# Attention and FFN layer on eight cores: the FFN weight's preparation moved into the loop over tiles, eight FFN tiles deferred

## The chip, the cores and the metric

The kernel runs on the eight cores of one Trainium2 chip. Each core does 4096 of the 32768 tokens and shares nothing with the others. The time is that of the device, in microseconds, of the slowest core.

## What is computed

A layer norm without weights, then attention over a window of seven neighbouring tokens with 16 heads of 64, and an FFN that is one product with a ternary weight; both are added to the input.

```python
def _layernorm(x, axis=-1, eps=1e-5): ...
def ste_quantize(w):
    scale = jnp.maximum(jnp.mean(jnp.abs(w)), EPS)
    return jnp.clip(jnp.round(w / scale), -1.0, 1.0)

xn = _layernorm(x, axis=-1)                       # x: (2, 16384, 1024) f32
# attention: q, k, v = xn @ w + b; 16 heads; each token sees offsets -3..3
scores = jnp.einsum('bhsd,bhskd->bhsk', q, k_win) * SCALE
attn = jax.nn.softmax(jnp.where(valid, scores, -jnp.inf), axis=-1)
out = jnp.einsum('bhsk,bhskd->bhsd', attn, v_win) @ w_o + b_o
# FFN: the scale is the mean of |weight|, a single number for the whole matrix
ffn = jnp.einsum('bsi,oi->bso', xn, w_ternary * scale)
x = x + out + ffn
```

## The kernel before

**Tiles and rings.** A core's 4102 rows (4096 and a margin of 3 on each side) are cut into 34 panels of 122 rows; a tile of 122 output rows needs a window of 128. Normalised, transposed activations `xnt`, keys `ktr` and queries `qme`, `qmo` (even and odd heads) are rings of four panels. `v_sb`, `ffn_sb`, `attok`, `atT`, `xr`, `osb` have two slots, `xl` (x for the layer norm) three. Five PSUM tensors: `p_tx` and `p_ta` for transposes, `p_qk` for all projections and for the FFN, `p_sc` for scores and attention output, `p_of` for the output projection. `p_qk` exists once, so each use waits for the evacuation of the last.

**Order.** The program is written out by hand: each `stage_` function appends instructions to five lists, one per engine, and each engine goes through its list in order. Waits are on counting semaphores; `evt` holds the count that an event reaches. The helper `dma(eng, chain, ...)` waits until the chain's earlier transfers have landed before it issues another, so one chain has one transfer in flight.

**Preamble.** SyncE loads three panels of x (122 rows of 4 KB each, 488 KB). Layer norm of panels 0 and 1 and the transposes of panel 0 follow. Then `emit_wcasts` loads wq, wk, wv, wo in 32 pieces of 512 KB over four slots of `wstage` and four chains, and ScalarE and VectorE cast them in turn. `emit_wf_prep` loads wf twice in four pieces of 1 MB: once for the sum of absolute values (L253), and, when the sum has gone over the partitions through two small matmuls (L266, L275), once for the ternary values, three VectorE instructions for each of eight blocks (L296, L300, L305), whose transposes (L313) and copies (L322) fill `wfT_b`. A row `brow` (bias of v through wo, plus bo) comes from 16 matmuls (L831). All this stands ahead of the loop in each engine's list.

**Loop.** Iteration s of 37 works on panel s and on tiles s-1, s-2 and s-3 in this order on TensorE: q and k projections of panel s (L475, bias L488), scores of tile s-1, heads 0 to 7 (L590), V projection of tile s-1 (L638), transposes of panel s+1 (L427) and of the attention output of tile s-2 (L666), scores, heads 8 to 15, FFN of tile s-1 (L692), output projection of tile s-2 (L721, L727), attention times V and row sums of tile s-1 (L748, L754). VectorE: reciprocals, `qmo` (L526), normalised attention (L779), residual addition `osb` of tile s-3 (L793), the mask multiplication `au_buf` (L614, one for each half of the heads), `xnt` (L441), part of the layer norm of panel s+2. ScalarE: `qme` (L522), `ktr` (L535), exponentials (L603), `v_sb` (L651), `atT` (L678), the rest of the layer norm, `ffn_sb` (L705). GpSimd adds `ffn_sb` to `osb` (L799) and stores it (L804). SyncE issues `xl` of panel s+3 (L336) and `xr`, the rows for the residual, of tile s-1 (L570); the latter waits for L793 of tile s-3.

## Time and profile before

| | us |
|---|---|
| median of 3 runs | 950.06 (949.19 to 950.79) |
| the profiled execution, its own time | 950.85 |
| its span, slowest core | 949.3 |
| spans of the eight cores | 941.7 to 949.3 |
| TensorE busy | 781.6 (82%) |
| VectorE, ScalarE, GpSimd busy | 324.7, 363.6, 98.9 |
| DMA, mean over the span | 77.07 MB, 81 GB/s |

The profile is of one execution on the slowest core. Its strip cuts the span into 40 slices of 23.7 us with the busy share of each in tenths. The chain of waits goes back from the last instruction to what released each step. The granted clock is given as a share of 2.4 GHz. A time in a row counts from the start of the span.

### The profile page before, as it was taken

To read this page: it belongs to the slowest core of one execution; us is meant where nothing else is said; L and a number is where in the kernel's file an instruction comes from. 1 tells how busy PE (TensorE), PEld (TensorE's weight loads), DVE (VectorE), ACT (ScalarE), POOL (GpSimd) and SP (SyncE) were. 2 spreads that over 40 slices of the span, in tenths; PEclk is the share of its full clock that TensorE was granted. 3 is DMA by queue.
4 is the path that set the end of the run, shared out by engine and by line. 5 is a ranking of instruction groups with operands and counts; after the bars stand their busy time and mean duration, and the time that the engine had idled before them with its cause. 6 is when DMAs were issued, how large, how long until landed. Compare 5 with 4: busy or idle time off the path is not lost.

```text
span 949.3 us, 21922 instructions; the slowest of 8 cores (941.7 to 949.3 us)
## 1 busy us (share of the span) xinstructions
PE 781.6 (82%) x8386; PEld 571.7 (60%) x8386; DVE 324.7 (34%) x566; ACT 363.6 (38%) x537; POOL 98.9 (10%) x72
## 2 busy tenths in 40 slices
PE   0000027899999999999999999999999999999984
PEld 0000014677777777777777777777777777777652
DVE  3112374223333333333333333333333333333221
ACT  0232113444444444444444444444444444444320
POOL 0000000001111111111111111111111111111112
PEclk9999999999999999999999999999999999999997
DMA  0479751101111111112211111111111111111211
GB/s 28 116 241 310 256 179 49 54 28 53 68 67 69 68 66 66 67 69 77 75 68 67 68 66 68 68 67 68 68 67 68 68 67 66 58 46 48 66 47 33
DMA packets 20531, 77.07 MB, mean 81 GB/s; under 512 B 1855, under 2 KB 1991, under 8 KB 20430
## 3 DMA queue, kind: packets, MB, share of 16 engines
q1 hardware_dynamic: 15582, 58.89, 17.4%
q0 software_dynamic: 4848, 16.78, 6.0%
q8 instruction: 70, 1.15, 0.5%
q14 instruction: 31, 0.25, 0.1%
HBM read 58.89 MB, written 16.78 MB: 80 GB/s over the span
## 4 chain that ended last, share of the span: by engine, by line
PE 80%; DMA 11%; DVE 4%; issue 2%; ACT 2%; DVEq 1%; POOL 0%; SPq 0%; ACTq 0%; POOLq 0%
PE p_qk L475 25%; PE p_of L727 13%; PE p_qk L692 13%; PE p_qk L638 13%; PE p_sc L748 5%; PE p_sc L590 3%; DMA xl<-x 3%; DMA wstage<-wq 2%; PE p_of L721 2%; PE p_qk L488 2%; DMA wstage<-wf 2%; PE p_qk L754 2%; PE p_tx L427 1%; DMA wstage<-wk 1%; DMA wstage<-wv 1%
## 5 line engine op out<-in xcount | busy, mean ns | idle before, releaser
L799 POOL TENSOR_TENSOR osb<-osb,ffn_sb 122x1024 f32<-122x1024 f32 (+1 forms) x34 | 80.1, 2355 | 822.8 <-DVE osb L793 803.5
L475 PE MATMUL p_qk<-xnt,wq_b 128*128 128x122 bf16 (+1 forms) x2176 | 128.2, 217 | 1.2 <-DVE xnt L441 1.2
L692 PE MATMUL p_qk<-wfT_b,xnt 128*122 128x512 bf16 (+1 forms) x544 | 123.6, 380 | 5.4 <-ACT v_sb L651 1.9
L727 PE MATMUL p_of<-wo_b,atT 128*122 128x512 bf16 (+1 forms) x544 | 126.7, 387 | 0.0
L638 PE MATMUL p_qk<-wv_b,xnt 128*128 128x512 bf16 (+1 forms) x544 | 124.6, 383 | 0.1
L475 PEld LDWEIGHTS p_qk<-xnt,wq_b 128*128 128x128 bf16 x2176 | 118.5, 98 | 9.0 <-issue 9.0
L475 PE MATMUL p_qk<-xnt,wk_b 128*128 128x122 bf16 (+1 forms) x2176 | 121.3, 215 | 0.4 <-ACT qme L522 0.4
L522 ACT CAST qme<-p_qk 64x488 bf16<-64x488 f32 (+1 forms) x86 | 39.2, 478 | 213.0 <-PE p_qk L488 205.8
L475 PEld LDWEIGHTS p_qk<-xnt,wk_b 128*128 128x128 bf16 x2176 | 115.7, 97 | 7.7 <-issue 7.6
L614 DVE TENSOR_TENSOR au_buf<-e_buf,mk_sb 128x976 bf16<-128x976 bf16 (+1 forms) x68 | 47.1, 693 | 207.4 <-ACT e_buf L603 207.4
L727 PEld LDWEIGHTS p_of<-wo_b,atT 128*122 128x122 bf16 (+1 forms) x544 | 70.5, 134 | 54.3 <-issue 16.0
L692 PEld LDWEIGHTS p_qk<-wfT_b,xnt 128*122 128x122 bf16 (+1 forms) x544 | 70.3, 134 | 48.9 <-issue 10.1
L638 PEld LDWEIGHTS p_qk<-wv_b,xnt 128*128 128x128 bf16 (+1 forms) x544 | 52.5, 99 | 57.3 <-issue 2.2
L266 PE MATMUL p_of<-stats,ones 128*1 128x1 f32 x2 | 0.2, 163 | 93.8 <-DVE stats L261 93.8
L603 ACT ACTIVATE e_buf<-p_sc,cst 128x976 bf16<-128x976 f32 (+1 forms) x68 | 71.8, 1056 | 7.5 <-PE p_sc L590 7.5
L535 ACT CAST ktr<-p_qk 128x488 bf16<-128x488 f32 (+1 forms) x86 | 39.7, 483 | 80.3 <-PE p_qk L475 80.3
L526 DVE CAST qmo<-p_qk 64x488 bf16<-64x488 f32 (+1 forms) x86 | 47.1, 565 | 64.8 <-PE p_qk L488 60.2
L748 PEld LDWEIGHTS p_sc<-v_sb,au_buf 128*122 128x122 bf16 (+1 forms) x544 | 63.1, 138 | 6.5 <-issue 3.9
L748 PE MATMUL p_sc<-v_sb,au_buf 128*122 128x64 bf16 (+1 forms) x544 | 64.4, 220 | 2.9 <-ACT ffn_sb L705 2.9
L651 ACT CAST v_sb<-p_qk 128x1024 bf16<-128x1024 f32 (+1 forms) x34 | 34.4, 1012 | 80.5 <-PE p_qk L638 80.5
L754 PE MATMUL p_qk<-ones128b,au_buf 128*122 128x1 bf16 (+1 forms) x544 | 64.3, 195 | 0.0
L754 PEld LDWEIGHTS p_qk<-ones128b,au_buf 128*122 128x122 bf16 (+1 forms) x544 | 62.4, 138 | 2.6
(77 smaller groups left out, 737.7 us busy)
## 6 DMA issues: line engine op xcount, KB each, us to landing
xl<-x SPq DMA_DIRECT2D x33, 488.0 KB
xr<-x SPq DMA_DIRECT2D x33, 488.0 KB
out<-osb POOLq DMA_DIRECT2D x33, 488.0 KB, 7.2
wstage<-wf SPq DMA_DIRECT2D x8, 1024.0 KB, 6.2
wstage<-wq SPq DMA_DIRECT2D x8, 512.0 KB, 11.6
wstage<-wk SPq DMA_DIRECT2D x8, 512.0 KB, 6.1
wstage<-wv SPq DMA_DIRECT2D x8, 512.0 KB, 5.6
wstage<-wo SPq DMA_DIRECT2D x8, 512.0 KB, 5.7
```

The source lines that it names most:

```text
L475: f = (lambda pp, m2, k2, c2, r2, wb2, st2, sp2: (lambda e: e.matmul(p_qk[0:128, c2:c2 + psz_of(pp)], wb2[0:128, k2 * H + 128 * m2: k2 * H ...
L522: f_e = (lambda pp, b2, qq, ww: (lambda e: e.copy(qap(qme)[0:64, 4 * b2:4 * b2 + 4, qq:qq + ww], p_qk[0:64, :].rearrange("p (b n) -> p b n ...
L526: f_o = (lambda pp, b2, qq, ww: (lambda e: e.tensor_copy(qap(qmo)[64:128, 4 * b2:4 * b2 + 4, qq:qq + ww], p_qk[64:128, :].rearrange("p (b ...
L535: f = (lambda pp, b2, rr, ww: (lambda e: e.copy(ktr_ap()[:, 4 * b2:4 * b2 + 4, rr:rr + ww], p_qk[:, :].rearrange("p (b n) -> p b n", b=2, ...
L603: inc("scalar", "s", (lambda ii, hf: (lambda e: e.activation(e_buf[0:wsz_of(ii), 8 * hf * TS:(8 * hf + 8) * TS] .rearrange("p (a b n) -> p ...
L614: inc("vector", "v", (lambda ii, hf, v2: (lambda e: e.tensor_tensor(au_buf[0:wsz_of(ii), :].rearrange("p (h n) -> p h n", h=NH, n=TS) [:, ...
L638: f = (lambda ii, k2, j2, r2: (lambda e: e.matmul(p_qk[0:wsz_of(ii), 512 * j2:512 * j2 + 512], xnt_ap()[:, k2, r2:r2 + wsz_of(ii)], wv_b[0 ...
L692: f = (lambda ii, k2, j2, q2: (lambda e: e.matmul(p_qk[0:tsz_of(ii), 512 * j2:512 * j2 + 512], xnt_ap()[:, k2, q2:q2 + tsz_of(ii)], wfT_b[ ...
L727: f = (lambda ii, k2, j2, a2: (lambda e: e.matmul(p_of[0:tsz_of(ii), 512 * j2:512 * j2 + 512], atT[:, :].rearrange("p (s c n) -> p s c n", ...
L748: f = (lambda ii, h2, v2: (lambda e: e.matmul(p_sc[0:tsz_of(ii), 64 * h2:64 * h2 + 64], au_buf[0:wsz_of(ii), TS * h2:TS * h2 + tsz_of(ii)] ...
L754: fd = (lambda ii, h2: (lambda e: e.matmul(p_qk[0:tsz_of(ii), 1008 + h2:1009 + h2], au_buf[0:wsz_of(ii), TS * h2:TS * h2 + tsz_of(ii)], on ...
L799: inc("gpsimd", "g", (lambda ii, s2, o2: (lambda e: e.tensor_add(osb[0:tsz_of(ii), o2 * H:(o2 + 1) * H], osb[0:tsz_of(ii), o2 * H:(o2 + 1) ...
```

## The change

Four things are changed together.

**Casts.** The 32 weight loads stay in one run on SyncE, with `xl` of panels 3 and 4 issued among them, after pieces 7 and 23. The casts go into the engines' lists at the start of iterations 0 (wq, wk), 1 (wv) and 2 (wo), on semaphores of their own (`cs`, `cv`). `brow` is made in iteration 2.

**wf.** Its preparation is cut into jobs, appended in iterations 3 to 7 behind the first half of the scores and the V projection: loads and absolute sums 0 and 1 in iteration 3, loads and sums 2 and 3 and the scale in iteration 4, blocks 0 and 1 in 5, blocks 2 to 4 in 6, blocks 5 to 7 in 7. The two small matmuls of the scale are replaced by four small transfers through a DRAM scratch tensor `scrv`, each in turn waited for.

**FFN of tiles 0 to 7.** It is taken out of iterations 1 to 8 and done in a run in iteration 8 (`flush_ffn_ladder`). `xnt` of tiles 0 to 4 is overwritten by then, so it is stored to DRAM (`scrx`, chain `x2`) in iterations 2 to 6 and loaded again into the space of `wtern`.

**Output of tiles 0 to 4.** Attention plus residual is stored to `out` in iterations 3 to 7 and in the run read back by GpSimd into `gsc` (under the name `pr_sb`), added to `ffn_sb` and stored again (`scr_pickup`).

```diff
+                jp = j - 4
+                wait("sync", "cs" if jp % 2 == 0 else "cv", jp // 2 + 1)
...
+                if j == 7 and NP > 3:
+                    stage_XLD(3)
+                    xld_done.add(3)
+                if j == 23 and NP > 4:
+                    stage_XLD(4)
+                    xld_done.add(4)
...
+            rng = {0: range(0, 16), 1: range(16, 24), 2: range(24, 32)}.get(s, range(0))
...
+        def _wf_scd1():
+            wait("sync", "v", evt[("wabs_c",)])
+            dma("sync", "sc", lambda e: e.dma_start(scrv_h[0, :], stats[:, 15:16]))
+            dma("sync", "sc", lambda e: e.dma_start(gsc[0:1, 0:128], scrv_h[0, :][None, :]),
+                key=("scd1",))
...
+        def _wf_scd2():
+            wait("sync", "v", evt[("srow",)])
+            dma("sync", "sc", lambda e: e.dma_start(scrv_h[1, :], gsc[0:1, 128:256]))
+            dma("sync", "sc", lambda e: e.dma_start(
+                sc_sc[:, 0:1], scrv_h[1, :].rearrange("(p n) -> p n", n=1)),
+                key=("scd2",))
...
+        S_F = min(8, NP + 2)
+        DEF = list(range(0, min(S_F, NT)))
+        SCR = list(range(0, max(0, S_F - 3)))
...
+        def emit_ffnev(j):
+            wait_ev("scalar", "t", ("ffn", j))
+            if j >= 2:
+                wait_ev("scalar", "s", ("ffnev", j - 2))
+                cons = ("ffnadd", j - 2) if (j - 2) in SCR else ("out2", j - 2)
+                wait_ev("scalar", "g", cons)
...
+        def x2_store(j):
...
+            dma("sync", "x2", (lambda jj, q2: (lambda e: e.dma_start(
+                scr_h[jj, :, :].rearrange("p (c n) -> p c n", c=8, n=TS),
+                xnt_ap()[:, :, q2:q2 + TS])))(j, qrc), key=("x2s", j))
...
+        def scr_pickup(jj):
+            wait_ev("gpsimd", "v", ("wtern", 7))
+            dma("gpsimd", "sp", (lambda j2: (lambda e: e.dma_start(
+                pr_sb[0:tsz_of(j2), :],
+                out_h[TS * j2:TS * j2 + tsz_of(j2), :])))(jj))
+            wait("gpsimd", "sp", 16 * (N_SCR + 2 * jj + 1))
+            wait_ev("gpsimd", "s", ("ffnev", jj))
+            inc("gpsimd", "g", (lambda j2: (lambda e: e.tensor_add(
+                pr_sb[0:tsz_of(j2), :],
+                pr_sb[0:tsz_of(j2), :],
+                ffn_sb[0:tsz_of(j2), (j2 % 2) * H:((j2 % 2) + 1) * H])))(jj),
+                key=("ffnadd", jj))
+            wait_ev("gpsimd", "g", ("ffnadd", jj))
+            dma("gpsimd", "sp", (lambda j2: (lambda e: e.dma_start(
+                out_h[TS * j2:TS * j2 + tsz_of(j2), :],
+                pr_sb[0:tsz_of(j2), :])))(jj))
...
+            for j in DEF:
+                if j - 2 in SCR:
+                    scr_pickup(j - 2)
...
+                if j >= 1:
+                    wait_ev("tensor", "s", ("ffnev", j - 1))
...
+            if s <= 2:
+                cast_flush(s)
...
+            flush_wf(s)
...
+            if s == S_F:
+                flush_ffn_ladder()
...
+            if 2 <= s <= S_F - 2 and (s - 2) in SCR:
+                x2_store(s - 2)
...
+                if ia >= S_F:
+                    stage_A_ffn(ia)
```

SyncE's list of before, from iteration 2 on, is a plain alternation; each xr waits for the VectorE addition two tiles back (`s_v`) and for its own predecessor (`s_lr`):

```order
50 L570 DMA xr<-x 122x1024 [waits s_lr]
51 L336 DMA xl<-x 122x1024 [waits s_s,s_v,s_lx]
52 L570 DMA xr<-x 122x1024 [waits s_v,s_lr]
53 L336 DMA xl<-x 122x1024 [waits s_s,s_v,s_lx]
54 L570 DMA xr<-x 122x1024 [waits s_v,s_lr]
```

Of the change, the same engine in iterations 3 and 4:

```order
46 L680 DMA xr<-x 122x1024 [waits s_v,s_lr]
47 L273 DMA wstage<-wf 128x2x1024 [waits s_cs,s_cv,s_w2]
48 L273 DMA wstage<-wf 128x2x1024 [waits s_cs,s_cv,s_w3]
49 L983 DMA scrx<-xnt 1024x1x122 [waits s_v,s_x2]
50 L442 DMA xl<-x 122x1024 [waits s_s,s_v,s_lx]
51 L680 DMA xr<-x 122x1024 [waits s_v,s_lr]
52 L273 DMA wstage<-wf 128x2x1024 [waits s_v,s_w2]
53 L273 DMA wstage<-wf 128x2x1024 [waits s_v,s_w3]
54 L297 DMA scrv<-stats 128x1 [waits s_v]
55 L298 DMA gsc<-scrv 1x128 [waits s_sc]
56 L315 DMA scrv<-gsc 1x128 [waits s_v,s_sc]
57 L316 DMA sc_sc<-scrv 128x1 [waits s_sc]
```

The loads of wf stand behind xr in the list, and the small transfers of the scale behind them.

VectorE before, one iteration from the residual addition to the layer norm:

```order
147 L793 TENSOR_TENSOR osb<-p_of,xr 122x1024 [waits s_t,s_lr,s_st,s_g]
148 L614 TENSOR_TENSOR au_buf<-e_buf,mk_sb 128x976 [waits s_s,s_t,s_v]
149 L441 COPY xnt<-p_tx 128x8x122 [waits s_t,s_v]
150 L367 TENSOR_REDUCE stats<-xl 122x1 [waits s_lx,s_v,s_s]
151 L372 TENSOR_SCALAR stats<-stats 122x1 [waits s_s]
```

The same place of the change, in iteration 5 (L920 is the residual addition, L724 the mask, L550 the xnt copy, L473 the sum of the layer norm):

```order
124 L920 TENSOR_TENSOR osb<-p_of,xr 122x1024 [waits s_t,s_lr,s_sp]
125 L724 TENSOR_TENSOR au_buf<-e_buf,mk_sb 128x976 [waits s_s,s_t,s_v]
126 L355 TENSOR_SCALAR gsc<-wstage,sc_sc 128x1024 [waits s_w2,s_v,s_sc]
127 L359 SCALAR_TENSOR_TENSOR gsc<-wstage,sc_sc,gsc 128x1024
128 L364 TENSOR_SCALAR wtern<-gsc,sc_sc 128x1024
129 L355 TENSOR_SCALAR gsc<-wstage,sc_sc 128x1024 [waits s_w2,s_v,s_sc]
130 L359 SCALAR_TENSOR_TENSOR gsc<-wstage,sc_sc,gsc 128x1024
131 L364 TENSOR_SCALAR wtern<-gsc,sc_sc 128x1024
132 L550 COPY xnt<-p_tx 128x8x122 [waits s_t,s_x2,s_v]
133 L473 TENSOR_REDUCE stats<-xl 122x1 [waits s_lx,s_v,s_s]
```

Between the mask and the xnt copy stand two ternary blocks, and ahead of them the wait for the load (`s_w2`).

GpSimd before did one addition and one store for each tile:

```order
7 L799 TENSOR_TENSOR osb<-osb,ffn_sb 122x1024 [waits s_v,s_s]
8 L804 DMA out<-osb 122x1024 [waits s_g,s_st]
```

In the run of iteration 8 it now has, after the reload of xnt, a read, an addition and a store for each of five tiles, all on the semaphore `s_sp`:

```order
13 L990 DMA wtern<-scrx 128x976 [waits s_t,s_x2,s_x3]
14 L1003 DMA gsc<-out 122x1024 [waits s_v,s_sp]
15 L1008 TENSOR_TENSOR gsc<-gsc,ffn_sb 122x1024 [waits s_sp,s_s]
16 L1014 DMA out<-gsc 122x1024 [waits s_g,s_sp]
17 L1003 DMA gsc<-out 122x1024 [waits s_v,s_sp]
18 L1008 TENSOR_TENSOR gsc<-gsc,ffn_sb 122x1024 [waits s_sp,s_s]
```

A read cannot be issued before the store ahead of it has landed.

## Rows read from the trace of the kernel before

**Rows 1.** The page's strip of 40 slices, TensorE matmuls, busy tenths.

```profile
PE   0000027899999999999999999999999999999984
```

**Rows 2.** Windows: length, busy of five engines, granted clock, DMA share, GB/s.

```profile
156.85:949.30 792.45, 766.36 (x8294) 562.45 (x8294) 269.59 (x490) 331.55 (x502) 98.73 (x68) 0.99 0.18 63
427.00:429.00 2.00, 2.00 (x26) 1.48 (x25) 0.00 (x0) 0.78 (x1) 0.00 (x0) 1.00 0.84 246
430.00:441.00 11.00, 11.00 (x99) 7.63 (x97) 2.49 (x8) 4.85 (x8) 0.00 (x0) 1.00 0.13 53
```

**Rows 3.** Chain of waits in order of time: start, duration, what.

```profile
1.06 1.95 DMA mk_sb<-mk
...
9.76 11.98 DMA xl<-x
...
35.31 17.74 DMA wstage<-wq
...
100.95 7.00 DMA wstage<-wf
...
156.85 1.82 PE p_qk L475 x32
...
213.70 1.74 PE p_qk L475 x32
...
236.24 1.74 PE p_qk L475 x32
```

**Rows 4.** Timeline up to 171 us: start, duration, instruction, idle before and its releaser.

```profile
75.47 0.69 DVE L227 CAST wk_b<-wstage 128x1024 bf16<-128x1024 f32 x1 [1.83 <-DMA wstage<-wk]
...
110.52 2.29 DVE L253 TENSOR_REDUCE absacc<-wstage 128x2 f32<-128x2048 f32 x1 [0.20 <-DMA wstage<-wf]
...
128.82 0.75 DVE L296 TENSOR_SCALAR gsc<-wstage,sc_sc 128x1024 f32<-128x1024 f32 x1
...
131.86 0.75 DVE L296 TENSOR_SCALAR gsc<-wstage,sc_sc 128x1024 f32<-128x1024 f32 x1
...
169.09 1.24 ACT L413 ACTIVATE xn_sb<-xl,stats 122x1024 bf16<-122x1024 f32 x1 [0.57 <-DVE stats L390]
```

**Rows 5.** Timeline and chain within one steady iteration, 416.5 to 439.

```profile
421.63 1.23 DVE L793 TENSOR_TENSOR osb<-p_of,xr 122x1024 f32<-122x1024 f32 x1
426.20 0.67 DVE L614 TENSOR_TENSOR au_buf<-e_buf,mk_sb 128x976 bf16<-128x976 bf16 x1 [3.34 <-ACT e_buf L603]
...
429.03 0.67 DVE L441 COPY xnt<-p_tx 128x976 bf16<-128x976 bf16 x1 [2.17 <-PE p_ta L666]
435.77 0.67 DVE L614 TENSOR_TENSOR au_buf<-e_buf,mk_sb 128x976 bf16<-128x976 bf16 x1 [2.64 <-ACT e_buf L603]
...
429.48 3.64 PE p_qk L692 x16
...
433.69 3.60 PE p_of L727 x16
```

**Rows 6.** Timeline of SyncE's own instructions, the DMA issues.

```profile
422.99 0.23 SPq L570 DMA_DIRECT2D xr<-x  x1
423.92 0.23 SPq L336 DMA_DIRECT2D xl<-x  x1
...
445.96 0.23 SPq L336 DMA_DIRECT2D xl<-x  x1
```

**Rows 7.** The page's GpSimd addition; DMA issues of 300 to 800, and 915 to 935.

```profile
L799 POOL TENSOR_TENSOR osb<-osb,ffn_sb 122x1024 f32<-122x1024 f32 (+1 forms) x34 | 80.1, 2355 | 822.8 <-DVE osb L793 803.5
...
out<-osb POOLq DMA_DIRECT2D x22, 488.0 KB, 7.2
...
out<-osb POOLq DMA_DIRECT2D x2, 488.0 KB, 3.9
```

**Rows 8.** The kernel's last tile: a window, columns as in rows 2, and the chain.

```profile
931.00:936.00 5.00, 4.34 (x10) 1.66 (x11) 0.00 (x0) 0.52 (x1) 2.88 (x2) 0.50 0.14 32
...
932.69 5.69 PE p_of L727 x16
```

More of the change, by code:

```diff
@@ L233, in emit_wf_prep @@
[L233 to L246 removed]
+        wf_state = {"wfT": -1, "ffnev": -1, "tat": -1}
@@ new lines, in _mk_p1ld, with _mk_wabs, f @@
+            return f
+        def _mk_wabs(j):
+            def f():
+                slot = j % 2
+                wait("vector", _wf_chain(j), evt[("wld", j)])
+                inc("vector", "v", (lambda sl, kk: (lambda e: e.tensor_reduce(
+                    absacc[:, 2 * kk:2 * kk + 2],
+                    wstage[:, 2 * sl * H:(2 * sl + 2) * H].rearrange("p (c n) -> p c n", c=2, n=H),
+                    AX.X, ALU.add,
+                    apply_absolute_value=True)))(slot, j), key=("wabs", j))
+            return f
@@ L328, in build_program, with flush_wf @@
+        for _c in range(2, 4):
+            _wfj(6, _mk_tern(_c))
+            _wfj(6, _mk_wtr(_c))
+        _wfj(6, _mk_p2ld(3))
+        _wfj(6, _mk_tern(4))
+        _wfj(6, _mk_wtr(4))
+        for _c in range(5, 8):
+            _wfj(7, _mk_tern(_c))
+            _wfj(7, _mk_wtr(_c))
+        wf_ptr = [0]
+        def flush_wf(s):
+            while wf_ptr[0] < len(wf_jobs) and wf_jobs[wf_ptr[0]][0] <= s:
+                wf_jobs[wf_ptr[0]][1]()
+                wf_ptr[0] += 1
         stash_P = {}
@@ L849, in build_program @@
             ir = s - 3
-            if s + 3 < NP:
+            if s + 3 < NP and s + 3 not in xld_done:
                 stage_XLD(s + 3)
+            if s <= 2:
+                cast_flush(s)
             if 0 <= io < NT:
```

449 lines of the change are left out of this document (281 added, 168 removed).

## The prediction, on record before the changed kernel ran

> **What bounds the kernel now.** I read the page's strip of slices first [rows 1]: TensorE is nearly idle in the first six of forty slices and full from the eighth on. The windows [rows 2] put the border at 156.85 us; from there TensorE is busy 766 of 792 us, so the loop is bound by its matmuls. The chain of waits [rows 3] then gives the calendar. Call the start of the projections of iteration s P(s). P(0) is at 156.85, P(3) at 213.70, P(4) at 236.24: the period is 22.54 us, so P(9) is at 213.70 + 6 x 22.54 = 348.9, and 600.4 us follow it. The hole before P(0) is what the change attacks. Its reason is in the timeline [rows 4]: the casts of wq and wk end at 76.2 us, yet P(0) stands behind wv, wo, two passes over wf and eight ternary blocks.
>
> Next I look at what is not on the path today but becomes so, the DMA queue of SyncE. The first xl load of 122 rows, alone, takes 11.98 us [rows 3]; 12.1 with the wake of the engine behind it is what I use. The windows [rows 2] say why: in 430 to 441 us the DMA share is 0.13, two of 16 engines, at 53 GB/s. A 488 KB load occupies these two for 10.4 to 11 us. xl and xr go out together once per period and follow one another on the same two engines: the issues of xl at 423.92 and 445.96 are 22 us apart [rows 6], and an issue waits for its predecessor to land. That pair of engines is busy 21 of 22.5 us, and whatever SyncE issues over all 16 engines finishes only after its two shares have passed the same line. The wq load behind the third xl shows it: 17.74 us for 512 KB [rows 3].
>
> **The change, part by part.** I work out the new P(s), on the profiled execution (950.85 us, span 949.3).
>
> (a) P(0). It now waits for wq and wk only, 76.2 us. But xl 3 is put between their loads, and costs its two engines 10.4 us in a stream that keeps all 16 busy. P(0) = 86.6: **-70.3 us**. The bounds are 76.2 and 88.3 (the 12.1 us).
>
> (b) Iterations 0 to 2. The casts of wv stand on ScalarE and VectorE ahead of the evacuations of P(1), and need loads that wait for casts that now stand behind LN of panel 2. Before, LN 2 ended at 170.33, 13.5 us after P(0) [rows 4]; 15.5 where P(0) begins at half clock. Four casts, four loads of about 1.7 us after a 5 us latency: the last cast is at +26, and the k projection, which needs the evacuated q bank, starts only then. P(2) comes at about +47. Loads of wo go behind xl 4 (10.4 us on the two engines), land at +36 to +41, and the last four are asked for at +46: cast at +56. The bias row (16 matmuls, an addition on VectorE) stands ahead of the output projection: P(3) at +80. Before it was 56.9: **+23.1**. Bounds: 0 if the casts' loads are always there in time, 30 if the restarts cost more.
>
> (c) Iterations 3 to 7. These have no FFN matmuls (3.64 us each) [rows 5], but that is worth little. Behind the V projection a chain runs through other engines: xnt at 429.03, LN, the second exp, au done at 436.44 [rows 5]. TensorE's own work, with the FFN, ends at 437.29. Without it the chain is what is late, and an iteration is 21.7, not 18.9. Times with a plus count from P(s); in [rows 5] P(s) is 236.24 + 8 x 22.54 = 416.5. Behind an obstacle on VectorE that ends at D, the chain is xnt to au, 7.4, and attnV, 1.8 (437.29 to the next P at 439.0): 9.3. Where transposes, a copy of wfT and the copy of atT behind it come between, I estimate 12.4. After a stall of over 2 us TensorE restarts at half clock: the granted clock is 0.50 (1.2 GHz) from 931 on, after a wait of 2 us, and 16 matmuls take 5.69 [rows 8] where the same 16 take 3.60 [rows 5]. With the few around them I take 2.7 us per restart. In each of these iterations SyncE issues xr after the residual addition (done at +6.4 [rows 5]), then 1 or 2 MB of wf at +6.9, behind xr on the two engines. So the first megabyte lands at 6.9 + 12.1 + 2.5 = +21.5, the second at +24.0 (2.5 apart, as the wf pair of before that landed at 107.95 [rows 3] and by 110.52 [rows 4]).
> - Iteration 3: xr 0, xl 5, xr 1, xl 6 and xr 2 all queue from +54 after P(0), 5 x 10.4 and the first x2 store of 2: the wf pair lands 113 and 115 after P(0), the second abs sum ends at 117, P(3) + 37. With 9.3 and 2.7: 49.0.
> - Iteration 4: abs sum done at 24.0 + 2.3 + 0.2; then two round trips through DRAM, four small transfers at 1.95 each [rows 3] and 1.2 of VectorE, all waited for on VectorE: 35.5. Iteration 47.5.
> - Iteration 5: 21.5 and two ternary blocks of 3.04 [rows 4], for which TensorE waits too, since the transposes stand in its order: 27.6 + 12.4 + 2.7 = 42.7.
> - Iteration 6: the third block needs a load issued in it, 24.6: 39.7. Iteration 7: three blocks from +10.5: 34.8.
>
> Sum 213.7 against 5 x 22.54: **+101.0**.
>
> (d) Iteration 8, the ladder. Eight FFN tiles stand in a row, from +12.9 on (V projection and v_sb). Each needs p_qk free, so each evacuation waits for its predecessor; and from the third on the evacuation waits for a slot of ffn_sb, so for GpSimd to have read the tile two before back from DRAM, added and begun the store. One buffer, one semaphore: read, add, store, in series. The add is 2.36 us [rows 7]; for the handovers I estimate 0.8. The store is 7.2 us with xl and xr about, 3.9 at the end of the kernel with that queue empty [rows 7]. After some 18 us of ladder the queue is empty, so I take 3.9, for the read too: a period of 11.0. The first pickup is issued at about +10 (after two small reloads), its addition ends at +19.6, the fifth at +63.8. Then evacuation 6, tile 7 at half clock (6.8 us): the ladder leaves TensorE at +72. Txn, LN, exp, au and attnV at the cold clock again: +84. P(9) = P(8) + 96.9 against 22.5: **+74.4**; 29 us of it is matmul work that left the eight earlier iterations, where it was mostly cover.
>
> The x2 stores (250 KB in short runs), the stores of tiles 0 to 4 and the reloads have slack of an iteration; I cost them at 2 us on the two engines in (c), and elsewhere at nothing. If a store took 10 us, the xnt copy behind it would wait: up to 5 x 8 us more. For (c) and (d) the bounds are the rivals 1 to 3 below.
>
> Sum: -70.3 + 23.1 + 101.0 + 74.4 = +128.2. P(9) at 477, and from there all is as before. 950.85 + 128 = 1079, and 0.8 less for the median of before: **1078 us**.
>
> **A rule beside it.** The trace shows 122-row loads on two engines. The Trainium skill, DMA: Bandwidth & Descriptors, section on why a DMA increments its semaphore by 16, says that a DMA uses the largest count up to 16 that divides its slowest dimension; for 122 that is 2, and the trace agrees. It also says that on GpSimd's path some direct copies use all 16 all the same: the out stores do (246 GB/s and a share of 0.84 while one moves, in 427 to 429 us [rows 2]). Which of the two the new read of out follows, no row shows.
>
> **The rivals.**
> 1. The wf loads do not stand behind xr. For it: the first wf load of before lands 7.00 us after its issue at 100.95 [rows 3]; nothing in the loop of before shows a 16-engine load behind an xr. Against: the wq load of 17.74 us. Then iterations 3 to 7 take 31, 40, 35, 35 and 35 us, 38 less, and (a) loses its 10.4: 1030.
> 2. The pickup read runs on two engines like xl: 12.1 instead of 3.9. Four periods of 8.2 more and 5 on the first: 38 more, 1116. The skill's page named above leaves room for it.
> 3. The pickups stay at 7.2 each way: 4 x 6.6 = 26 more, 1104.
> 4. Faster than before: TensorE is never held by the moved work, because VectorE (idle two thirds of the loop) does it in gaps. Then only (a) and (b) count, -47: 904. It decides where the extra of iterations 3 to 8 falls below 47 us. I find 175. VectorE alone needs 34 us for sums and blocks, TensorE waits for each block in order, and four pickup periods are 44 with only 24 of matmuls beside them. The whole mechanism would have to be a different one.
>
> **How the numbers follow.** Forecast, 1053 to 1103: 0.56. Rival 1: 0.17. Rival 2: 0.12. Rival 3: 0.08. Something between 953 and 1020, still slower: 0.04. Rival 4: 0.03. The range 1028 to 1110 leaves out rival 2, the unnamed rest and rival 4, 0.19. About 0.2% is what a measurement of this kernel can tell: faster 0.03, same 0.01, slower 0.96.
>
> **What would show it.** P(0) (first q projection after the wk casts) near 87 us, with an xl load among the weight loads. VectorE idle for 10 us or more ahead of each absacc reduction and of the first gsc of iterations 5 and 6, released by the wf DMA; a landing of wf near 15 to 17 us after issue, not 7. Two waits of 4 us for scrv. In the ladder TensorE at 0.50, ScalarE's ffn_sb copies released by GpSimd, 11 us apart. P(9) near 477 and then a period of 22.5. Wrong would be: wf landing in 7 us (rival 1), pickups 19 us apart (rival 2), or a loop after P(9) with another period, which no part of this allows for.

## The result and the profile after

The changed kernel takes **1106.7 us** (median of 10 runs, 1101.8 to 1113.0); the kernel before took 949.6 beside it (10 runs, 948.5 to 951.1). The ratio is **1.1655, interval 1.1631 to 1.1679**: slower by 157 us. Forecast was 1078 with 1028 to 1110 around it. The direction is right, the size is 29 us short, and the time lies in the upper end of the range. The times here and below leave out executions in which the cores of one die ran at a lower clock than the others. The profiled execution took 1103.6 us; its slowest core has a span of 1102.1, the others 1087.3 to 1101.0.

The page's strip, TensorE busy and granted clock in 40 slices of 27.6 us, and the page's line on the wf loads:

```profile
PE   0005586432384783569999999999999999999984
...
PEclk9999688675785897679999999999999999999987
...
wstage<-wf SPq DMA_DIRECT2D x8, 1024.0 KB, 18.7
```

TensorE works from slice 4 on, where before it began in slice 6 [rows 1], but it is about half idle until slice 19, and its mean clock is lower in most of these slices. From slice 19 on the strip is that of before. A megabyte of wf lands 18.7 us after its issue (median), where 7.00 stood in the chain before [rows 3].

The calendar comes from VectorE's timeline. The reciprocal of tile s-2 starts within 0.4 us of P(s), so I take its starts as the starts of iterations 2 to 10:

```profile
142.18 0.25 DVE L893 RECIPROCAL recip<-p_qk 122x16 f32<-122x16 f32 x1
166.55 0.26 DVE L893 RECIPROCAL recip<-p_qk 122x16 f32<-122x16 f32 x1 [4.32 <-PE p_qk L878]
212.20 0.26 DVE L893 RECIPROCAL recip<-p_qk 122x16 f32<-122x16 f32 x1 [3.86 <-PE p_qk L878]
271.68 0.26 DVE L893 RECIPROCAL recip<-p_qk 122x16 f32<-122x16 f32 x1 [3.86 <-PE p_qk L878]
317.64 0.26 DVE L893 RECIPROCAL recip<-p_qk 122x16 f32<-122x16 f32 x1 [2.34 <-PE p_qk L878]
360.50 0.26 DVE L893 RECIPROCAL recip<-p_qk 122x16 f32<-122x16 f32 x1 [3.57 <-PE p_qk L878]
393.20 0.26 DVE L893 RECIPROCAL recip<-p_qk 122x16 f32<-122x16 f32 x1 [2.34 <-PE p_qk L878]
496.84 0.26 DVE L893 RECIPROCAL recip<-p_qk 122x16 f32<-122x16 f32 x1 [3.26 <-PE p_qk L878]
521.57 0.26 DVE L893 RECIPROCAL recip<-p_qk 122x16 f32<-122x16 f32 x1 [2.75 <-PE p_qk L878]
```

Set against the forecast, step by step:

| | forecast | measured |
|---|---|---|
| P(0) | 86.6 | 85.9 |
| P(3) after P(0) | 80 | 80.7 |
| iterations 3, 4, 5, 6, 7 | 49.0, 47.5, 42.7, 39.7, 34.8 | 45.7, 59.5, 46.0, 42.9, 32.7 |
| iteration 8 | 96.9 | 103.6 |
| P(9) | 477 | 496.8 |
| from P(9) to the end of the span | 600.4 | 605.3 |

The chain of waits (start, duration, what) shows what the long iterations are made of:

```profile
62.24 14.92 DMA wstage<-wk
...
85.89 3.41 PE p_qk L585 x32
...
177.66 20.99 DMA wstage<-wf
...
220.76 19.12 DMA wstage<-wf
...
242.60 9.91 DMA scrv<-stats
...
252.58 3.60 DMA gsc<-scrv
...
257.26 1.12 DMA scrv<-gsc
...
258.44 1.95 DMA sc_sc<-scrv
...
280.45 17.18 DMA wstage<-wf
...
324.30 18.22 DMA wstage<-wf
...
417.39 8.02 DMA gsc<-out
...
433.03 4.58 DMA gsc<-out
...
478.48 6.51 PE p_qk L805 x16
```

Each of iterations 3 to 6 has one wf load of 17 to 21 us in the chain. In iteration 4 the four small transfers of the scale follow it. From 417 on it is the pickups: read, addition, store, read. The view of waits for 200 to 500 us (total, times, longest) names the same three obstacles from the side of the engines that wait:

```profile
PE p_sc L872 <- DVE au_buf L724: 62.6, 3, 36.6
...
ACT ffn_sb L821 <- POOL gsc L1008: 57.4, 5, 12.2
...
PE p_ta L379 <- DVE wtern L364: 40.6, 8, 16.1
...
DVE gsc L355 <- DMA wstage<-wf: 23.0, 2, 13.9
```

Its first line holds TensorE's longest waits, for the mask `au_buf`: 36.6 us in iteration 4 and 24.0 in iteration 3, because the second mask of an iteration stands in VectorE's list behind the xnt copy, and that one behind the absolute sums and the scale. TensorE also waits 41 us for ternary blocks, and VectorE, ahead of those blocks, for wf. ScalarE waits 57 us for GpSimd before it may copy the next FFN tile out of `p_qk`, five times. In iterations 3 to 7 together TensorE is busy 120 of 227 us, at a mean clock of 0.71 (columns as in [rows 2]):

```profile
166.55:393.20 226.65, 119.82 (x1209) 89.72 (x1207) 72.49 (x109) 53.66 (x77) 3.89 (x7) 0.71 0.27 80
```

### The profile page after: what moved, and what is told of

Its sections match the earlier page's. It is cut to its first block, busy times and chain, and to the rows that moved or that the text cites. A ratio compares the mean times of both kernels' runs of the same rounds, so it can differ in the third digit from the quotient of the medians.

```text
span 1102.1 us, 22136 instructions; the slowest of 8 cores (1087.3 to 1102.1 us)
## 1 busy us (share of the span) xinstructions
PE 819.4 (74%) x8382; PEld 595.7 (54%) x8382; DVE 323.9 (29%) x567; ACT 364.8 (33%) x537; POOL 106.8 (10%) x87
## 4 chain that ended last, share of the span: by engine, by line
PE 64%; DMA 21%; DVE 4%; issue 4%; ACT 3%; POOL 2%; DVEq 1%; SPq 1%; ACTq 0%; POOLq 0%
PE p_qk L585 21%; PE p_of L850 11%; PE p_qk L748 9%; PE p_qk L805 9%; DMA wstage<-wf 7%; PE p_sc L872 4%; DMA gsc<-out 2%; DMA wstage<-wq 2%; DMA xl<-x 2%; DMA wstage<-wk 2%; PE p_sc L700 2%; PE p_of L844 2%; PE p_qk L598 2%; PE p_qk L878 2%; POOL gsc L1008 1%
## 5 line engine op out<-in xcount | busy, mean ns | idle before, releaser
L585 PE MATMUL p_qk<-xnt,wq_b 128*128 128x122 bf16 (+1 forms) x2176 | 137.4, 225 | 62.1 <-DVE wk_b L251 57.3
L585 PEld LDWEIGHTS p_qk<-xnt,wq_b 128*128 128x128 bf16 x2176 | 127.5, 102 | 70.5 <-issue 70.4
L850 PE MATMUL p_of<-wo_b,atT 128*122 128x512 bf16 (+1 forms) x544 | 132.6, 400 | 0.0
L805 PE MATMUL p_qk<-wfT_b,xnt 128*122 128x512 bf16 (+1 forms) x464 | 112.5, 398 | 23.8 <-ACT ffn_sb L821 19.3
L872 PE MATMUL p_sc<-v_sb,au_buf 128*122 128x64 bf16 (+1 forms) x544 | 68.4, 225 | 69.6 <-DVE au_buf L724 69.4
L934 POOL TENSOR_TENSOR osb<-osb,ffn_sb 122x1024 f32<-122x1024 f32 (+1 forms) x28 | 65.9, 2354 | 518.2 <-DVE osb L920 499.0
L724 DVE TENSOR_TENSOR au_buf<-e_buf,mk_sb 128x976 bf16<-128x976 bf16 (+1 forms) x68 | 46.5, 684 | 210.1 <-ACT e_buf L713 210.1
L805 PEld LDWEIGHTS p_qk<-wfT_b,xnt 128*122 128x122 bf16 (+1 forms) x464 | 62.9, 141 | 65.9 <-issue 35.4
L878 PE MATMUL p_qk<-ones128b,au_buf 128*122 128x1 bf16 (+1 forms) x544 | 68.2, 198 | 0.0
L645 ACT CAST ktr<-p_qk 128x488 bf16<-128x488 f32 (+1 forms) x86 | 39.7, 483 | 84.5 <-PE p_qk L585 84.5
L878 PEld LDWEIGHTS p_qk<-ones128b,au_buf 128*122 128x122 bf16 (+1 forms) x544 | 66.3, 145 | 2.2
L550 DVE COPY xnt<-p_tx 128x976 bf16<-128x976 bf16 (+1 forms) x34 | 22.5, 661 | 141.3 <-PE p_tx L533 139.1
## 6 DMA issues: line engine op xcount, KB each, us to landing
wstage<-wf SPq DMA_DIRECT2D x8, 1024.0 KB, 18.7
```

Source lines behind the costliest of these rows:

```text
L585: f = (lambda pp, m2, k2, c2, r2, wb2, st2, sp2: (lambda e: e.matmul(p_qk[0:128, c2:c2 + psz_of(pp)], wb2[0:128, k2 * H + 128 * m2: k2 * H ...
L645: f = (lambda pp, b2, rr, ww: (lambda e: e.copy(ktr_ap()[:, 4 * b2:4 * b2 + 4, rr:rr + ww], p_qk[:, :].rearrange("p (b n) -> p b n", b=2, ...
L724: inc("vector", "v", (lambda ii, hf, v2: (lambda e: e.tensor_tensor(au_buf[0:wsz_of(ii), :].rearrange("p (h n) -> p h n", h=NH, n=TS) [:, ...
L805: f = (lambda ii, k2, j2, q2: (lambda e: e.matmul(p_qk[0:tsz_of(ii), 512 * j2:512 * j2 + 512], xnt_ap()[:, k2, q2:q2 + tsz_of(ii)], wfT_b[ ...
L850: f = (lambda ii, k2, j2, a2: (lambda e: e.matmul(p_of[0:tsz_of(ii), 512 * j2:512 * j2 + 512], atT[:, :].rearrange("p (s c n) -> p s c n", ...
L872: f = (lambda ii, h2, v2: (lambda e: e.matmul(p_sc[0:tsz_of(ii), 64 * h2:64 * h2 + 64], au_buf[0:wsz_of(ii), TS * h2:TS * h2 + tsz_of(ii)] ...
```

## The experiments

Two theories go in. The first is the prediction's: the x loads of 122 rows occupy two DMA engines, and wf, which uses all sixteen, finishes behind them; without FFN matmuls the chain through LN and the second exponential is late; the pickups go in series. The second stands for its rivals: that wf is slow for another reason, that the FFN matmuls left a real gain in iterations 3 to 7, and that the pickups are held by two slow engines. Differences below are differences of the ratios to the runs of before beside them, times 950 us.

**Experiment 1.** In the changed kernel every x load, `xl` and `xr`, is issued as 112 and 10 rows.

```diff
-            dma("sync", "lx", (lambda pp, s2: (lambda e: e.dma_start(
-                xl[0:psz_of(pp), s2 * H:(s2 + 1) * H],
-                x_h[TS * pp:TS * pp + psz_of(pp), :])))(p, p % 3),
+            for rn in (16 * (psz_of(p) // 16), psz_of(p) % 16):
+                if rn:
+                    inc("sync", "lx", (lambda pp, s2, a, n: (lambda e: e.dma_start(
+                        xl[a:a + n, s2 * H:(s2 + 1) * H],
+                        x_h[TS * pp + a:TS * pp + a + n, :])))(p, p % 3, r0, rn),
```

> The change, with each 122-row load of x (xl and xr) issued as two, 112 rows and 10 rows, and nothing else altered. Queue theory (122 rows run on two engines, and wf waits behind them): a load of x lands in about 4 us, the three first ones no longer hold the weights, P(0) moves from 86 to about 53, wf lands 7 to 8 us after its issue instead of 19, iterations 3 to 6 lose some 12 us each, and the time falls by about 90, to near 1017. Rival (the wf loads were slow for another cause, such as traffic of the other cores or the scattered stores of xnt): x loads may land sooner, but wf stays near 15 to 19 us and the time falls by less than 40.

Measured: ratio 1.0969 (1.0919 to 1.1020), 1043 us, 65 less. P(0) came at 58.4 instead of 85.9, and iterations 3 to 7 took 198 us instead of 227. Of the page, the wf loads:

```profile
wstage<-wf SPq DMA_DIRECT2D x8, 1024.0 KB, 10.3
```

So the two-engine loads are the cause of most of what the 18.7 us had above 7, and of 27 us ahead of P(0). They are not all of it: 90 us less and a landing of 7 to 8 were expected, and the landing went to 10.3. Two loads of 1 MB are still issued behind an `xr`, and their volume has to pass.

**Experiment 2.** The change with the wf loads issued at the top of each iteration, ahead of `xl` and `xr`.

```diff
+        top_jobs = {3: [_mk_p1ld(0), _mk_p1ld(1)], 4: [_mk_p1ld(2), _mk_p1ld(3)],
+                    5: [_mk_p2ld(0), _mk_p2ld(1)], 6: [_mk_p2ld(2)]}
...
-            _wfj(3, _mk_p1ld(_j))
...
+            for _f in top_jobs.get(s, []):
+                _f()
             if s + 3 < NP and s + 3 not in xld_done:
```

> The change, with the wf loads of iterations 3 to 6 (all but the last) issued by SyncE at the top of the iteration, ahead of xl and xr instead of behind xr. Queue theory: they are issued about 7 us sooner and no xr of the same iteration stands ahead of them, so in iterations 4 to 6 wf is in when VectorE comes to it at +10.5 and these give back 10 to 14 us each; iteration 3 gives back less, since older xl and xr are still queued: 30 to 50 us less in all, near 1065. Rival (wf is slow for a cause of its own): 7 us less at most in each of four iterations, under 28 in all.

Measured: 1.1203 (1.1170 to 1.1237), 1064 us, 43 less. Iterations 3, 5 and 6 fell to 25.8, 32.8 and 33.5; iteration 3, expected to give back least, gave back most. The landing of wf fell from 18.7 to 12.2 us (the page's median). But the edit did more than change the order in the queue. In the changed kernel SyncE comes to wf only when `xr` ahead of it may be issued, which waits for the residual addition; at the top of the iteration it is held by nothing of that iteration. The first pairs went out at 157.24 and 183.59, which is 10 us before P(3) and P(4), instead of 7 to 8 us after them. That is 17 to 18 us earlier and not the 7 of the expectation, so the bound of 28 us for the rival doesn't hold, and this run can't tell the place in the queue from the earlier issue. Experiment 1, which leaves the order alone, can. Iteration 4 rose to 65.2; its chain says why:

```profile
209.57 24.86 DMA scrv<-stats
...
234.50 1.51 DMA gsc<-scrv
...
238.19 9.16 DMA sc_sc<-scrv
```

What now stands behind `xl` (issued at 195.1) and `xr` (201.0) on the two engines is the first small transfer of the scale, half a kilobyte. Part of the 24.86 us is its own: in the changed kernel the same transfer took 9.91, with a DMA share of 0.01 beside it. The 9.16 us of the last transfer stand on this core only; on the other seven it took 1.9 to 2.0.

**Experiments 3, 9 and 12** ask what the absent FFN matmuls are worth in the loop, in the kernel before. All three leave out 14 of the 16 FFN matmuls of every tile. Experiment 3 does nothing else:

```diff
-            for kc in range(8):
+            for kc in (0,):
```

> The kernel before, with 2 of the 16 FFN matmuls of each tile left (the other 14 are left out, so the FFN output is not computed in full). My reading of iterations without FFN (the chain V projection, LN, exp, au is what is late): taking 14 x 0.227 = 3.2 us of matmul out of each iteration shortens the period from 22.54 to 21.7 only, and a wait of TensorE for au_buf of over 2 us appears ahead of the attention products. Rival (TensorE's own work is what counts): the period falls to about 19.4, and the time by 34 x 3.2 = 108 us.

Measured: 980.7 us in one run, against 950.9 for the kernel before (median of six runs). Some 108 us of TensorE's work are gone (14 of 16 matmuls of 3.64 us [rows 5], 34 times), and the kernel is **slower by 30 us**. Neither theory had that. One iteration, chain of waits:

```profile
427.35 3.02 PE p_qk L475 x32
...
446.89 1.06 ACT e_buf L603
...
448.18 0.68 DVE au_buf L614
...
449.20 0.21 PE p_sc L748
```

VectorE's copy of xnt in the same iteration, from its timeline, and TensorE's wait for the mask in the whole run:

```profile
441.43 0.67 DVE L441 COPY xnt<-p_tx 128x976 bf16<-128x976 bf16 x1 [2.16 <-PE p_ta L666]
```

```profile
PE p_sc L748 <- DVE au_buf L614: 71.4, 30, 2.8
```

TensorE now waits some 2.4 us in each iteration for the second exponential and the mask. The next 32 matmuls take 3.02 us where they took 1.74 before [rows 3], at a granted clock of 0.53, nearly all at 1.2 GHz (window of 427.35 to 430.40). The period is 23.8 us, 2.1 above the prediction's 21.7: xnt starts 14.1 us after the iteration and not 12.5 (1.3 of the 1.6 is the restart), and attention times V takes 2.3 after the mask and not 1.8. The chain between the two is 7.4 as forecast. In the kernel before, the FFN matmuls fill this gap.

Experiment 9 puts the second exponential ahead of the layer norm in the lists:

```diff
                 stage_O_tat(io)
+            if 0 <= ia < NT:
+                stash_sc2.pop(ia)(1)
             if s + 2 < NP:
...
-                stash_sc2.pop(ia)(1)
                 stage_A_ffn(ia)
```

> The kernel before with 2 of 16 FFN matmuls (as e3; the other 14 are left out) and the second exponential and its mask multiplication ahead of the layer norm of panel s+2 in the lists of ScalarE and VectorE, in every iteration. In e3 the period was 23.8 us, above the 22.54 with all matmuls: TensorE waited 2 us for au_buf ahead of attnV in each iteration and did the next 32 matmuls at half clock (3.0 instead of 1.8 us). Chain theory: with the exponential first, au_buf is ready some 5 us sooner, the wait and the half clock go, and the period falls to what the matmuls take, about 19.3: a time near 950 - 34 x 3.2 = 842. Rival (the clock falls for another cause, such as less work per iteration): the period stays above 22.

Measured: 1023 us in the profiled execution, a miss by 180. TensorE waited 100 us in 31 waits for the copy to `ffn_sb`. The chain of an iteration:

```profile
482.23 1.10 ACT e_buf L603
...
488.90 1.00 ACT ffn_sb L705
...
490.04 0.21 PE p_sc L748
```

The exponential is early as meant, but the copy to `ffn_sb` was left behind the layer norm, and the row sums of the attention (L754) write to `p_qk`, which this copy frees. I had looked at one tenant of the buffer only. Experiment 12 moves both:

```diff
+            if 0 <= ia < NT:
+                stash_sc2.pop(ia)(1)
+                stage_A_ffn(ia)
             if s + 2 < NP:
...
-            if 0 <= ia < NT:
-                stash_sc2.pop(ia)(1)
-                stage_A_ffn(ia)
```

> As e9 (2 of 16 FFN matmuls; the other 14 are left out), with the two matmuls and the copy to ffn_sb ahead of LN as well. In e9 the exponential was no longer late, but the copy to ffn_sb was behind LN on ScalarE, and attnV waits for it because both use p_qk: the wait grew from 2 to 5 us and the period to 25. Chain theory: with nothing that attnV needs behind LN, the wait before it goes, TensorE stays at full clock and the period is what the matmuls take, 19.3 to 19.8: a time of 840 to 860. Rival (fewer matmuls per iteration lower the clock or expose another chain): the period stays above 21.

Measured: 853.4 us in one run, against 951.8 beside it. Two reciprocals of its loop:

```profile
442.56 0.26 DVE L769 RECIPROCAL recip<-p_qk 122x16 f32<-122x16 f32 x1 [1.32 <-PE p_qk L754]
462.27 0.26 DVE L769 RECIPROCAL recip<-p_qk 122x16 f32<-122x16 f32 x1 [1.33 <-PE p_qk L754]
```

The period is 19.71 us, near TensorE's own 22.54 - 3.64 = 18.9 and two matmuls; the mean clock of the slowest core is 0.987 instead of 0.933. Same arithmetic, 127 us apart from experiment 3: with the lists as they were, the chain and the clock behind it, not the matmuls, set an iteration without FFN.

**Experiment 4.** The edit of experiment 1 alone in the kernel before.

> The kernel before, with the same two-part loads of x and nothing else altered. Queue theory: the three x loads at the start take about 4 us each instead of 12, the third no longer stands ahead of the weights, and the weights come about 24 us sooner; all behind them in the preamble is a chain, so P(0) moves from 157 to about 132 and the time falls by about 24, to near 926. The loop does not change, since its x loads have slack. Rival (the first 34 us are a start-up cost of the memory, not of the two engines): less than 5 us.

Measured: 0.9799 (0.9773 to 0.9824), 931 us. The start of the first projections moved from 156.85 to 137.85 us, 19 where 24 were expected; the period stayed at 22.5. The windows (columns as in [rows 2]) of before:

```profile
14.00:20.00 6.00, 0.00 (x0) 0.00 (x0) 5.14 (x9) 0.00 (x0) 0.00 (x0) 1.00 0.13 53
20.00:26.00 6.00, 0.00 (x0) 0.00 (x0) 1.82 (x6) 3.02 (x5) 0.00 (x0) 1.00 0.09 29
```

and of this run:

```profile
14.00:20.00 6.00, 0.00 (x0) 0.00 (x0) 5.15 (x2) 0.00 (x0) 0.00 (x0) 1.00 0.35 90
20.00:26.00 6.00, 0.00 (x0) 0.00 (x0) 3.45 (x15) 4.24 (x7) 0.00 (x0) 1.00 0.95 258
```

In 14 to 20 us x is being loaded in both; the DMA share goes from 0.13 (two of sixteen) to 0.35, and from 20 us on the weights already have nearly all sixteen. The rule that the prediction quoted (the Trainium skill, DMA: Bandwidth & Descriptors, section Why a DMA increments its semaphore by 16 and not by 1) would give 112 rows sixteen engines; the trace agrees that they are more than two, and in a window of large and small loads doesn't show their number. The 19 us lie in the preamble alone, since in the loop of before nobody waits for x.

**Experiment 5.** The change with the five reads of `out` issued ahead of the run of FFN tiles, each into its own buffer and on its own semaphore; GpSimd then only adds and stores.

```diff
+        def scr_read(jj):
...
+            dma("gpsimd", pk_ch[jj], (lambda j2: (lambda e: e.dma_start(
+                pk_buf(j2),
+                out_h[TS * j2:TS * j2 + TS, :])))(jj), key=("pkr", jj))
...
+                for jj in SCR:
+                    scr_read(jj)
```

> The change, with the five reads of out issued by GpSimd right after the two x2 reloads of iteration 7, each into a buffer of its own (four slots of wstage, free by then, and gsc) with a semaphore of its own; additions and stores as before, no store waited for. Serial-pickup theory: the 12.2 us period of the run of FFN tiles goes; each tile takes its 3.64 of matmul and 1.1 of evacuation, and iteration 8 falls from 103.6 to about 65 to 70: 34 to 38 us less in all. Rival (the run is held by the reloads of xnt, 5.8 us each, and by half clock): 15 us less or fewer.

Measured: 1.1304 (1.1281 to 1.1328), 1074 us, 33 less. Iteration 8 took 69.1 us instead of 103.6. ScalarE's copies out of `p_qk`, in its timeline:

```profile
434.20 1.01 ACT L822 COPY ffn_sb<-p_qk 122x1024 f32<-122x1024 f32 x1 [5.13 <-POOL wstage L1019]
439.30 1.01 ACT L822 COPY ffn_sb<-p_qk 122x1024 f32<-122x1024 f32 x1 [4.09 <-PE p_qk L800]
```

These two are 5.1 us apart, 16 matmuls and a copy, and all eight 5.0 to 7.1, where the changed kernel has 12.0 to 13.2 from the second to the seventh. The serial pickup is confirmed as the price of iteration 8. What is left, 69 us against 22.5, is the run of eight tiles over one `p_qk` and the chain behind it.

**Experiment 6.** The scale by two matmuls as before, instead of through DRAM.

```diff
-            dma("sync", "sc", lambda e: e.dma_start(scrv_h[0, :], stats[:, 15:16]))
...
+            inc("tensor", "t", lambda e: e.matmul(
+                p_of[0:1, 8:9], ones128[:, 0:1], stats[:, 15:16], start=True, stop=True),
+                key=("abs_mm",))
```

> The change, with the scale made by the two small matmuls of the kernel before (in iteration 4, into p_of) instead of the four transfers through DRAM. Iteration 4 took 59.5 us; from the last absolute sum (242.3) to the scale on all partitions (260.8) it spent 18.5, where the kernel before spent 1.9 (122.3 to 124.2). Theory: 16 to 17 us less in all. Rival (the wait only uncovers another): less than 8.

Measured: 1.1509 (1.1461 to 1.1556), 1092 us, 14 less. Iteration 4 fell from 59.5 to 47.0, 12.5 where 16 to 17 were expected. The same step in its chain, two matmuls instead of four transfers:

```profile
247.39 0.20 PE p_of L299 x2
...
247.98 0.55 PE p_of L308 x2
```

**Experiment 7.** The four transfers kept, but the first vector of 128 floats is written with 512 bytes from one to the next.

```diff
+    scrp_h = nc.dram_tensor("scrp", [128, 128], F32, kind="Internal").ap()
...
-            dma("sync", "sc", lambda e: e.dma_start(scrv_h[0, :], stats[:, 15:16]))
+            dma("sync", "sc", lambda e: e.dma_start(scrp_h[:, 0:1], stats[:, 15:16], allow_slow_non_contiguous=True))
```

> The change, with the 128 numbers of the first scale transfer written 512 bytes apart in DRAM (and read back from there as 128 single numbers) instead of next to each other. In the change that write of 512 bytes took 9.91 us and the read of it 3.60. If the write is slow because 128 writes of 4 bytes fall into one short stretch of DRAM, it falls to 3 us or less here; if it is slow for being 128 writes of 4 bytes wherever they go, it stays near 10. The read will be 3 to 5.

Measured: 1098.9 us in one run. The write's place in the chain:

```profile
243.78 1.44 DMA scrp<-stats
```

1.44 us instead of 9.91, with the same number of 4-byte pieces and the same place in the list. The other cores repeat it: 1.4 to 2.5 us on the eight cores of this run, 6.2 to 9.9 on those of the changed kernel. Iteration 4 took 52.3 instead of 59.5. The write is slow when the 128 pieces fall into one stretch of 512 bytes. What in the memory does that, the run doesn't tell. The Trainium skill, DMA: Bandwidth & Descriptors, section Specifications, says that a transfer below 512 bytes is a read-modify-write; that would hold for both layouts, so it can't be the difference by itself.

**Experiment 10.** The repairs of experiments 1, 5 and 6 together.

> The change with the repairs of e1 (x loads in two parts), e5 (reads of out ahead) and e6 (scale by matmuls) together. If the three costs are separate they add: 1107 - 62 - 33 - 15 = 997, still slower than before, since the DVE work inside iterations 3 to 7, the missing cover of the FFN and half clock remain. If they overlap (each repair was worth more because another wait was there) the sum is smaller: above 1010.

Measured: 1.0521 (1.0486 to 1.0556), 1000 us. The three single gains are 65 + 33 + 14 = 112, together they give 108: they are nearly independent. By its calendar (P(3) 136.9, P(8) 322.1, P(9) 395.8 against 213.8, 326.5, 349.1 of before) the early start is 77 us ahead at P(3), iterations 3 to 7 give back 73 and iteration 8 another 51. With each of the three found costs repaired, the plan still loses 50 us: from P(3) to P(8) TensorE is busy 121 of 185 us at a mean clock of 0.75, and its longest waits there are still for ternary blocks (29 us) and for the mask (17).

**Experiments 8 and 11** ask rival 4: is moving the preamble into the loop wrong, or this way of doing it? Both defer the FFN of three tiles only, so that no tile goes through DRAM, put all casts into iteration 0 and wf into iterations 0 to 3, and take the repairs of experiments 1 and 6. The second exponential stands ahead of the layer norm while the FFN is deferred.

```diff
-        S_F = min(8, NP + 2)
+        S_F = 3
...
-            rng = {0: range(0, 16), 1: range(16, 24), 2: range(24, 32)}.get(s, range(0))
+            rng = {0: range(0, 32)}.get(s, range(0))
...
+            (0, "E"): [_mk_wabs(0), _mk_p1ld(2), _mk_wabs(1), _mk_p1ld(3)],
+            (1, "A"): [_mk_wabs(2), _mk_p2ld(0), _mk_wabs(3), _mk_p2ld(1)],
+            (1, "E"): [_wf_absc, _wf_scd1],
```

> A version meant to be faster than both: x loads in two parts; all 32 casts ahead of the evacuations of P(0), the loop begun there; absolute sums of wf in iterations 0 and 1, scale by matmuls, ternary blocks in iterations 2 and 3 with the transposes one block later than VectorE; FFN of only three tiles deferred (their xnt is still in its ring), so no scratch in DRAM; and in iterations 0 to 3 the second exponential stands ahead of LN. Theory: the evacuation of P(0) at about 83, the run of three FFN tiles at about 160 to 170, P(4) at about 185 to 195 (236.4 before, 217.3 with split loads): near 900 to 910. Rival (VectorE's 34 us of wf work hold TensorE as in the change): P(4) at 215 or later, no gain over the 931 of the split loads alone.

Measured: 0.9735 (0.9716 to 0.9753), 925 us, short of what was expected. P(4) is at 210.0, outside the forecast: iterations 2 and 3 took 40 and 50 us. In iteration 2 TensorE stands 7.4 us ahead of the output projection, because VectorE has a third ternary block and the layer norm ahead of the bias row; in iteration 3 its waits for ternary blocks come to 5.9 us. The mean clock is 0.84 and 0.83. Experiment 11 spreads the blocks finer, makes the bias row ahead of the second block, and takes the third VectorE instruction of each block away by scaling the FFN's result in ScalarE's copy:

```diff
-                inc("vector", "v", (lambda w2: (lambda e: e.tensor_scalar_mul(
-                    wtern[:, w2 * H:(w2 + 1) * H], gsc[:, 0:H], sc_sc[:, 3:4])))(wsl),
...
-            inc("scalar", "s", (lambda ii, s2: (lambda e: e.copy(
+            inc("scalar", "s", (lambda ii, s2: (lambda e: e.activation(
...
-                p_qk[0:tsz_of(ii), 0:H])))(j, j % 2),
+                p_qk[0:tsz_of(ii), 0:H], AF.Identity,
+                scale=sc_sc[0:tsz_of(ii), 3:4])))(j, j % 2),
```

> e8 with three edits: the ternary block is two VectorE instructions instead of three (values -1, 0, 1 in bf16, the scale applied in the evacuation of the FFN, block 2.1 us instead of 3.05); blocks begin at the top of iteration 2, between its evacuations; the bias row is made behind the V projection of iteration 2 instead of behind LN. In e8 iteration 2 took 40 and iteration 3 took 50 us, TensorE waiting for blocks. Theory: the run of three FFN tiles starts at about 165 instead of 185, P(4) at about 190 instead of 210, the time near 905. Rival (what holds iterations 2 and 3 is the chain through LN and half clock, not the blocks): 8 us or less.

Measured: **0.9633 (0.9619 to 0.9648), 914.4 us, the fastest kernel of this study**. Its calendar and chain:

```profile
175.03 6.21 PE p_qk L781 x16
...
199.85 1.74 PE p_qk L556 x32
```

P(4) is at 200.0 against 236.4 of before, 36 us, and that is the gain of 35. Experiment 4 has 19 of them without any of this, so the early start itself is worth 16. Against experiment 8 the three edits together gave 10 us, where 20 were expected; iteration 2 went from 40.1 to 32.3 and iteration 3 only from 49.8 to 47.5. No run separates them. The first FFN tile still runs at half clock, 6.21 us.

## Why the prediction was right and where it was short

**What bounds the kernel, and (a).** Right. P(0) came 0.7 us from the forecast, with one xl load among the weight loads as its reason: wk took 14.92 us in one wait. Experiment 1 splits it and gives P(0) 58.4, 27.5 us less. Of these, 19 are the three first x loads (experiment 4), which leaves 8.5 for this one, near the 10.4 of the forecast.

**(b).** Right in sum, with one step in another place. The last cast of wv ended 28.3 us after P(0) (forecast 26), the last of wo at +56.4 (forecast +56). But P(2) came at +56.3 and not at +47: VectorE has the casts of wo ahead of the reciprocal, which must read `p_qk` before P(2) may write it. I had let only the output projection wait for wo. As TensorE then had everything ready, iteration 2 was short. From the last cast of wo to P(3) it is 24.3 us, forecast 24, and so P(3) came within a microsecond.

**(c).** The mechanism was right: experiment 1 takes 28 us out of these iterations with nothing changed but the engines that x occupies. Two terms were mis-sized. The **scale's round trip** is the larger one: I took 1.95 us for each of four transfers from a row of a plain load of a mask; the write of 128 adjacent floats took 9.91 and the read behind it 3.60. With the absolute sums done 3.6 us later than forecast in that iteration, it took 59.5 instead of 47.5. The **wf landing** was forecast at 14.6 to 17.1 us after issue and was 17.2 to 21.0: counted from P(s), it came 4.5 us late in iteration 5 (1.9 of it the issue) and 3.4 in iteration 6, which took 3.3 and 3.2 us more. Iterations 3 and 7 came 3.4 and 2.1 under. Sum of (c): 13.0 too little.

That the absent FFN is no gain was right for a stronger reason than I gave. The chain bound of 21.7 us omitted the restart behind its own wait: experiment 3 shows 23.8, more than the period with the FFN. I had used restarts only behind VectorE's obstacles.

The restart itself was put too simply, as what follows a wait of over 2 us. In the changed kernel two waits for ternary blocks are nearly alike, 2.24 us ahead of 331.29 and 2.33 ahead of 334.22. The eight transposes behind the first took 0.61 us at a granted clock of 1.00, those behind the second 1.01 us at 0.50. And in experiment 3 the attention products right behind the wait still run at full pace (0.19 to 0.22 us each); the 32 matmuls after them are the slow ones. So the 2.7 us per restart aren't a fixed price, and no run here tested them by themselves.

**(d).** The mechanism was right: 57.4 us of waits of ScalarE for GpSimd, and experiment 5 removes 35 of the 103.6 us. The size was short by 6.7. Counted as the prediction did, from the start of the FFN tiles at P(8) + 12.9 = 406.1, the fifth addition ended at +71.1 and not +63.8; from there to P(9) it was 19.6 us, forecast 20.2. GpSimd's timeline gives one period:

```profile
433.03 0.53 POOL L1003 DMA_DIRECT2D gsc<-out  x1 [3.25 <-DMA out<-gsc]
437.81 2.33 POOL L1008 TENSOR_TENSOR gsc<-gsc,ffn_sb 122x1024 f32<-122x1024 f32 x1 [4.25 <-DMA gsc<-out]
440.77 0.53 POOL L1014 DMA_DIRECT2D out<-gsc  x1 [0.63 <-POOL gsc L1008]
445.18 0.52 POOL L1003 DMA_DIRECT2D gsc<-out  x1 [3.88 <-DMA out<-gsc]
```

Read 4.6 + 0.2, addition 2.3, handover 0.6, store 3.85, next issue 0.6: 12.15 against 11.0. The read was costed at the store's 3.9, the handovers at 0.8 instead of 1.4. The first read took 8.02, beside a reload. The stores of `xnt` take 19.5 us each on SyncE's queue (the page's median), and no wait of the trace names them: that they cost nothing was right, for the reason given, an iteration of slack in iterations that were twice as long.

**From P(9) on.** I let all be as before. Iteration 9 begins with TensorE at half clock (24.7 instead of 22.5). Then the period is that of before up to the end of the kernel. There 1.1 us more lie in the last full iteration, whose 16 matmuls of the V projection took 6.17 us where they took 5.32 before, and 1.6 behind its reciprocal, most of it after the last store is issued. The median lies 3.1 us above the profiled execution. The last two I can't explain by any row.

The whole miss: 13.0 in (c), 6.7 in (d), 4.9 behind P(9), 3.1 between execution and median, and 0.8 that the forecast took off: 28.5 of 28.7 us.

**The rivals.** Rival 1 fell: wf landed late, and experiment 1 says why; its price for iterations 3 to 7 (38 us) was near what experiment 1 gave (28), which still has the volume of x to pass. Rival 2 fell: the read took 4.6 us and not 12. The DMA share while such a read moves is 0.49 (445.80 to 449.60 us), where an xl load has 0.13. The Trainium skill (DMA: Bandwidth & Descriptors, section Why a DMA increments its semaphore by 16 and not by 1) has an exception for some direct copies on GpSimd's path, which the prediction quoted; by this trace it holds for this read too. Rival 3 fell, with store 3.9 and read 4.6 for the pickups behind the first. Its 1104 lies close to the measured time by chance. Rival 4 was wrong for this kernel and right for the idea: with three deferred tiles, no tile through DRAM and the order of experiment 11, the early start gains 16 us beyond the 19 of the split x loads. What it needed is what I named, that VectorE's work doesn't hold TensorE in order; even there it does in part (130 us from 70 to 200 have 89 us of matmuls at a clock of 0.81, by the windows of experiment 11).

**Open.** Why experiment 1 left wf at 10.3 us and not 7 is argued from volume, not shown. How much of the gain of experiment 2 is the place in the queue and how much the earlier issue is open. No run separated the restarts of the clock from the waits ahead of them in iterations 3 to 7.
